# A graph layer on one core: all edge rows scattered in the score stage

## The chip, the core and the metric

The kernel runs on one core of a Trainium2 chip: TensorE (PE, with its weight loads PEld), VectorE (DVE), ScalarE (ACT), GpSimd (POOL) and SyncE (SP), each with its own instruction queue, and 16 DMA engines that all queues share. The metric is the device time of one execution in microseconds, the median of the runs.

## The reference

There are 6250 nodes of 256 features and 200000 edges. An edge goes from a source (`src`, random) to an owner (`dst`, sorted), and carries three times. Layer norms and the typed output layer stand around this core, which is what the stages below compute:

```python
K, Q, V = [typed_linear(x, W, b, node_type) for W, b in ((Wk, bk), (Wq, bq), (Wv, bv))]
e0, e1, e2 = [cos(log(edge_attr[:, i] + 1)[:, None] * w_time + b_time) for i in (0, 1, 2)]
def edge_msgs(Kn, Qn, Vn, ek, eq):
    k = concatenate([Kn, ek], 1).reshape(-1, H, DK)          # H = 4, DK = 56
    q = concatenate([Qn, eq], 1).reshape(-1, H, DK)
    att = einsum('ehd,ed->eh', k, q.sum(axis=1)) / sqrt(DK)
    return att, concatenate([Vn, ek], 1).reshape(-1, H, DK)
att, v = edge_msgs(K[row], Q[col], V[row], e1, e2)           # row = src, col = dst
att_i, v_i = edge_msgs(K[col], Q[row], V[col], e2, e1)
att, att_i = seg_softmax(att, col, n), seg_softmax(att_i, row, n)
res = concatenate([(v * att[:, :, None]).reshape(-1, H * DK), e0], 1)
res_i = concatenate([(v_i * att_i[:, :, None]).reshape(-1, H * DK), e0], 1)
agg = segment_sum(res, col, n) + segment_sum(res_i, row, n)
```

So each edge gives one row of 256 values to the node that it ends in (direction 0) and one to the node that it starts from (direction 1), each weighted by its own softmax.

## The kernel before

Edges are laid out as 1664 tiles of 128. In a tile all edges belong to one group of 128 nodes, so that a sum over a tile is a matmul with a 128x128 one-hot. Work goes in rounds of 8 tiles (`G`), 208 rounds (`NS`) a stage. There are two orders of the edges, one by owner (direction 0) and one by source (direction 1). The stages run one after the other, with a barrier of all engines between them:

- `group_nodes`, `project`: node types, and a table in DRAM with K, Q and V of each node.
- `sort_edges` (`count_owners`, `place_edges`): counts, and for each edge its slot in both orders. The edges' records are scattered to owner order. A record holds also its slot in source order (`SLOT`); unused slots of `bys` are filled with empty rows here, by scatters of `k.padslot`.
- `exchange`, the score stage, works in owner order. A round loads records (SP, L905), gathers the sources' table rows (POOL, L942, eight indirect DMAs of 128 rows of 1888 bytes, into one of three `row` buffers), takes the owners' rows from an SBUF table by matmul (PE, L1062; ACT copies them out, L986 and L987), makes the time embeddings (ACT, L1000 to L1005) and both scores (DVE, L1113 to L1118). SP stores the direction 0 rows to `spill` (L922) and the scores to `runs` (L924). The direction 1 rows, 264 words each with value, scores, source and slot, are collected in `pb`, two buffers, and SP stores them linearly, in owner order, to `mid` (L926).
- `to_runs`, `softmax`, `weights`, `aggregate` for direction 0, then the same four for direction 1. `aggregate` is the sum: SP loads rows (L1446), ACT makes the one-hots (L1487 to L1495), DVE weighs the rows (L1508), PE sums them (L1469), DVE adds to the total (L1518).
- `store_sums`, `output`.

Direction 1 needs its rows by source, in `bys`. In the kernel before, `forward` (L1129) does this, one indirect DMA on POOL for 128 rows, after `mid` has been reloaded: 16 rounds (`AHEAD`) inside the first `softmax`, where ACT issues the loads ahead of its exponentials, and 192 rounds inside the first `aggregate`. There SP first issues the loads of 32 rounds (`LEAD`, L1441) ahead of its own row loads, and then one load a round; from round 160 on there are none left. After round 160 ACT waits for all scatters (`scores_back`) and loads the direction 1 scores, 20 bytes of each of the 212992 rows, in eight DMAs (L1483). Only then does it make the one-hots of the last 48 rounds.

The order of work on each engine is written out by hand; every wait is a semaphore in the engine's queue. In `exchange` POOL's queue is, per round n: wait for the score of round n-1 (`s_sco`), wait for the indices of round n+2 (`s_of`) and for the store of the row buffer (`s_v`), then eight gathers of round n+2. ACT's `owners` waits until the `pb` buffer that it is to fill has been stored (`s_mid`).

Of the kernel before, what the change touches and what calls it, by code (L numbers as in the profile page):

```python
# [8 lines left out]
F32 = mybir.dt.float32  # L9
# [6 lines left out]
P = 128  # L16
# [6 lines left out]
class Sizes:  # L23


    def __init__(self, x, dst, Wk, Wa, w_time):
# [37 lines left out]
        self.AHEAD = 16  # L64
        self.LEAD = 32
# [340 lines left out]
def sort_edges(nc, k, S, src, dst, edge_attr, recs, otile1, bys):  # L406
# [3 lines left out]
    with ExitStack() as ctx:  # L410
        s = Scope(nc, ctx, "sort")
        own = s.sb("own", [P, 2, CT])
# [430 lines left out]
def exchange(nc, k, S, w_time, b_time, table, recs, spill, mid, runs):  # L843
# [16 lines left out]
    with ExitStack() as ctx:  # L860
# [7 lines left out]
        pb = [s.sb(f"pb{n}", [P, G, RC]) for n in range(2)]  # L868
# [9 lines left out]
        prod = s.sb("prod", [P, G, H, DK])  # L878
# [7 lines left out]
        s_u, s_tu, s_fr, s_as, s_mid = [[s.sem(f"{n}{h}") for h in range(2)] for n in ("u", "tu", "fr", "as", "mid")]  # L886
        s_row, s_v = [[s.sem(f"{n}{h}") for h in range(R)] for n in ("row", "v")]
# [14 lines left out]
        def _(sp):  # L902
# [13 lines left out]
            def step(n, i, j, left):  # L916
# [8 lines left out]
                sp.wait_ge(s_sco, n + 1)  # L925
                sp.dma_start(mid[:, bass.ds(n * G, G), :], pb[h][:]).then_inc(s_mid[h], 16)  # L926
            rounds(sp, step)
            for h in range(2):
                sp.wait_ge(s_as[h], 16 * (NS // 2))
                sp.wait_ge(s_mid[h], 16 * (NS // 2))  # L930
# [4 lines left out]
        def _(pool):  # L935
# [9 lines left out]

            def step(n, i, j, left):
                if left >= 2:
                    pool.wait_ge(s_sco, n)
                    gathers(n + 2, i, j + 2)
            gathers(0, 0, 0)  # L950
            gathers(1, 0, 1)
            rounds(pool, step)

        @block.scalar
        def _(act):
# [11 lines left out]
            def owners(n, i, j):  # L967
                h, q = ring(j, 2), ring(j, 4)
                act.wait_ge(s_mid[h], 16 * turn_of(i, j, 2, PER))
                act.wait_ge(s_as[h], 16 * turn_of(i, j, 2, PER))  # L970
                nc.scalar.activation(pb[h][:, :, S.SLOTC].bitcast(I32), rec[q][:, :, S.SLOT].bitcast(I32), ACT.Copy)
                nc.scalar.activation(pb[h][:, :, S.SC + H:S.SC + H + 1], rec[q][:, :, S.SRC:S.SRC + 1], ACT.Copy)
                nc.scalar.activation(at[h][:, :, H:H + 1], rec[q][:, :, S.OWN:S.OWN + 1], ACT.Copy).then_inc(s_own, 1)
# [7 lines left out]
            def gathered(n, j):  # L981
                h = ring(j, 2)
                act.wait_ge(s_sco, n - 1 if not isinstance(n, int) else max(n - 1, 0))
                for t in range(G):
                    act.wait_ge(s_gat, n * G + t + 1)
                    nc.scalar.activation(pb[h][:, t, 0:PROJ], pG[t % 4][:, 0:PROJ], ACT.Copy)  # L986
# [9 lines left out]
            def cosines(n, i, j):  # L996
# [3 lines left out]
                nc.scalar.activation(pb[h][:, :, PROJ:PROJ + 2 * TD], frac[:, :, 0:2 * TD], ACT.Sin, scale=-2 * math.pi)  # L1000
# [79 lines left out]
        def _(dve):  # L1080
            nc.vector.memset(tab[:, NO - 1, :], 0.0).then_inc(s_clr, 1)
            for h in range(2):
                nc.vector.memset(pb[h][:, :, S.RCW:RC], 0.0)
# [14 lines left out]
            def step(n, i, j, left):  # L1098
                h, q = ring(j, 2), ring(j, R)
                link, n_link = chain(dve, s_dve, n * 4)  # L1100
# [11 lines left out]
                dve.wait_ge(s_ev, (n + 1) * G)  # L1112
                link(nc.vector.tensor_tensor(c[:, :, QT:DK], c[:, :, QT:DK], c[:, :, DK + PROJ:QKE], ALU.add))  # L1113
# [5 lines left out]
                assert n_link[0] == 4  # L1119
# [13 lines left out]
def softmax(nc, k, S, d, att_d, keys, alpha_d, mid=None, bys=None):  # L1133
# [5 lines left out]
    with ExitStack() as ctx:  # L1139
# [17 lines left out]
        if bys is not None:  # L1157
            s_turn = s.sem("turn")
            pb = [s.sb(f"pb{n}", [P, S.G, S.RC]) for n in range(8)]
            s_pb, s_sc = [[s.sem(f"{n}{j}") for j in range(8)] for n in ("pb", "sc")]  # L1160
# [40 lines left out]
        @block.gpsimd  # L1201
        def _(pool):
            if bys is not None:
                for n in range(S.AHEAD):
                    pool.wait_ge(s_pb[n % 8], 16 * (n // 8 + 1))
                    pool.sem_inc(s_turn, 1)
                    for t in range(S.G):
                        forward(nc, S, pb[n % 8], t, bys).then_inc(s_sc[n % 8], 16)
                for n in range(8):
                    pool.wait_ge(s_sc[n], 16 * S.G * (S.AHEAD // 8))  # L1210

        @block.scalar
        def _(act):
            if bys is not None:
                for n in range(S.AHEAD):
                    if n >= 8:
                        act.wait_ge(s_sc[n % 8], 16 * S.G * (n // 8))
                    nc.scalar.dma_start(pb[n % 8][:], mid[:, n * S.G:(n + 1) * S.G, :]).then_inc(s_pb[n % 8], 16)
# [166 lines left out]
def aggregate(nc, k, S, s2, d, rows_v, head, al, total, crd=None, mid=None, bys=None):  # L1385
# [16 lines left out]
    ONLY = S.LEAD if bys is not None else 0  # L1402
    SKIP = S.AHEAD if bys is not None else 0
    BOTH = NS - ONLY - SKIP if bys is not None else 0
    if bys is not None:
        pb = [s2.sb(f"pb{n}", [P, G, S.RC]) for n in range(4)]
# [417 lines left out]
```

## Time and profile before

| | us |
|---|---|
| runs, median of 3 | 11923.16 |
| lowest to highest | 11920.98 to 11970.68 |
| profiled execution | 11958.76 |
| its span in the trace | 11956.7 |

```profile
## 1 busy us (share of the span) xinstructions
PE 7581.8 (63%) x33184; PEld 5391.1 (45%) x33185; DVE 6391.6 (53%) x13112; ACT 4234.1 (35%) x12997; POOL 6309.1 (53%) x5432
## 2 busy tenths in 40 slices
PE   3787777777777747777777771034455526499555
PEld 1276666677666633333333331023343314377322
DVE  1096555555555537777777775022233326788533
ACT  0101222222222226666666661022233315488311
POOL 3302555555555548888888885677777760000122
PEclk6655555555555558888898885567677768799755
DMA  1110000000000028888988887567777779588410
```

Section 1 is each engine's busy time. Section 2 cuts the span in 40 slices of 299 us; a digit is the busy share in tenths, and the row PEclk is TensorE's granted clock. Slices 15 to 24 are the score stage, 25 is the first softmax, 26 to 34 the first sum, 35 to 37 the second softmax and sum. POOL counts only while an instruction of it runs; the gap that it needs between two of them is idle time here.

### The profile page before, as it was taken

To read this page: it belongs to the slowest core of one execution; us is meant where nothing else is said; L and a number is where in the kernel's file an instruction comes from. 1 tells how busy PE (TensorE), PEld (TensorE's weight loads), DVE (VectorE), ACT (ScalarE), POOL (GpSimd) and SP (SyncE) were. 2 spreads that over 40 slices of the span, in tenths; PEclk is the share of its full clock that TensorE was granted. 3 is DMA by queue.
4 is the path that set the end of the run, shared out by engine and by line. 5 is a ranking of instruction groups with operands and counts; after the bars stand their busy time and mean duration, and the time that the engine had idled before them with its cause. 6 is when DMAs were issued, how large, how long until landed. Compare 5 with 4: busy or idle time off the path is not lost. (4 is left out here: it accounts for less than half of the span.)

```text
span 11956.7 us, 138038 instructions
## 1 busy us (share of the span) xinstructions
PE 7581.8 (63%) x33184; PEld 5391.1 (45%) x33185; DVE 6391.6 (53%) x13112; ACT 4234.1 (35%) x12997; POOL 6309.1 (53%) x5432
## 2 busy tenths in 40 slices
PE   3787777777777747777777771034455526499555
PEld 1276666677666633333333331023343314377322
DVE  1096555555555537777777775022233326788533
ACT  0101222222222226666666661022233315488311
POOL 3302555555555548888888885677777760000122
PEclk6655555555555558888898885567677768799755
DMA  1110000000000028888988887567777779588410
GB/s 64 36 42 5 6 6 6 6 6 6 6 6 6 6 96 308 308 304 304 306 306 302 304 293 222 179 242 267 256 278 274 272 195 165 175 258 259 157 34 16
DMA packets 1338916, 1878.44 MB, mean 157 GB/s; under 512 B 413200, under 2 KB 1138683, under 8 KB 1285261
## 3 DMA queue, kind: packets, MB, share of 16 engines
q1 hardware_dynamic: 861902, 1184.16, 29.1%
q0 software_dynamic: 261440, 671.33, 17.5%
q10 hardware_dynamic: 215424, 21.56, 2.3%
q14 instruction: 132, 1.08, 0.0%
q8 instruction: 18, 0.29, 0.0%
HBM read 1160.18 MB, written 747.87 MB: 160 GB/s over the span
## 5 line engine op out<-in xcount | busy, mean ns | idle before, releaser
L1469 PE MATMUL sum_pS<-sum_row,sum_oh 128*128 128x260 f32 x6656 | 1854.8, 440 | 1577.1 <-issue 1347.2
L942 POOL DMA_INDIRECT exch_row<-table,exch_of x1664 | 2293.7, 1378 | 625.7 <-issue 549.9
L792 POOL DMA_INDIRECT recs<-place_rec,place_addr x1568 | 1617.6, 1032 | 1572.4 <-DVE place_rec L772 1101.3
L1469 PEld LDWEIGHTS sum_pS<-sum_row,sum_oh 128*128 128x128 f32 x6656 | 1435.6, 221 | 1996.0 <-issue 1737.2
L1129 POOL DMA_INDIRECT bys<-sum_pb x1536 | 1695.0, 1104 | 592.7 <-issue 490.6
L1062 PE MATMUL exch_pG<-exch_tab,exch_ohT 128*128 x3328 | 1607.5, 638 | 475.2 <-ACT exch_kc L987 281.0
L704 PE MATMUL place_pL<-place_cur,place_t_lo 128*128 128x49 f32 x6272 | 1423.7, 409 | 71.8 <-issue 69.2
L1508 DVE TENSOR_TENSOR sum_row<-sum_row,agg_al 128x1792 f32<-128x1792 f32 x416 | 840.7, 2021 | 1165.4 <-DMA sum_row<-spill 850.0
L704 PEld LDWEIGHTS place_pL<-place_cur,place_t_lo 128*128 128x128 f32 x6272 | 1397.0, 332 | 84.5 <-issue 82.1
L1062 PEld LDWEIGHTS exch_pG<-exch_tab,exch_ohT 128*128 128x128 f32 x3328 | 722.4, 227 | 1331.0 <-issue 1330.0
L752 DVE SCALAR_TENSOR_TENSOR place_junk<-place_pB,place_own_g,sort_tri 128x128 bf16<-128x128 f32 x3136 | 887.9, 346 | 289.6 <-DMA table<-proj_kv,proj_idx 261.8
L1495 ACT ACTIVATE sum_oh<-sum_off 128x1024 f32<-128x1024 f32 x416 | 439.6, 1057 | 1686.5 <-DMA soft_key<-keys 794.8
L1491 ACT ACTIVATE sum_off<-kept_ramp,sum_neg 128x128 f32<-128x128 f32 x3328 | 1017.5, 388 | 0.0
L760 DVE TENSOR_TENSOR place_prod<-place_pL,sort_oh_hi 128x392 f32<-128x392 f32 x392 | 345.0, 880 | 1111.3 <-remote 863.6
L643 ACT ACTIVATE place_t_lo<-place_pT 128x1024 f32<-128x1024 bf16 x392 | 399.4, 1019 | 1426.3 <-remote 1288.8
L1619 POOL MEMSET out_xr<- 128x1024 f32 x2 | 1.8, 951 | 1399.3 <-POOLq L112 1399.3
L695 PE MATMUL place_pB<-place_rows,sort_sel 64*128 64x128 bf16 x3136 | 469.0, 301 | 369.4 <-issue 369.4
L1518 DVE TENSOR_TENSOR edge_acc<-edge_acc,sum_pS 128x260 f32 x832 | 351.7, 423 | 653.0 <-DMA soft_key<-keys 279.2
L986 ACT ACTIVATE exch_pb<-exch_pG 128x192 f32<-128x192 f32 x1664 | 562.3, 338 | 274.5 <-PE exch_pG L1062 179.4
L987 ACT ACTIVATE exch_kc<-exch_pG 128x248 f32<-128x248 f32 x1664 | 641.9, 386 | 0.0
L708 PE MATMUL place_pC<-sort_oh_hi,sort_oh_lo 128*128 128x49 bf16 x3136 | 425.2, 276 | 213.9 <-issue 204.7
L647 ACT ACTIVATE place_cur<-place_pC 128x392 f32<-128x392 f32 x394 | 195.2, 496 | 1007.5 <-PE place_pC L708 528.5
(290 smaller groups left out, 11019.2 us busy)
## 6 DMA issues: line engine op xcount, KB each, us to landing
mid<-exch_pb SPq DMA_DIRECT2D x208, 1056.0 KB
spill<-exch_row SPq DMA_DIRECT2D x208, 1024.0 KB
sum_row<-spill SPq DMA_DIRECT2D x208, 1024.0 KB
sum_row<-bys SPq DMA_DIRECT2D x208, 1024.0 KB
sum_pb<-mid SPq DMA_DIRECT2D x192, 1056.0 KB
exch_row<-table,exch_of POOLq DMA_INDIRECT x1664
recs<-place_rec,place_addr POOLq DMA_INDIRECT x1568
bys<-sum_pb POOLq DMA_INDIRECT x1536
```

Of the source, the lines that this page charges most:

```text
L695: last = nc.tensor.matmul(pB[b][:, t, :], sel[:, u % 2 * 16 + u // 2 * LN + 4 * b + t, :], rows[:, par, :], start=True, stop=True)
L704: last = nc.tensor.matmul(pL[u % 2][:, t * NO:(t + 1) * NO], t_lo[:, u % 2, t, :], cur[:, d, t * NO:(t + 1) * NO], start=True, stop=True)
L752: last = nc.vector.scalar_tensor_tensor(out=junk[:, b, t, :], in0=pB[b][:, t, :], scalar=own_g[:, par, d, c:c + 1], in1=tri[:], op0=ALU.is ...
L792: nc.gpsimd.indirect_dma_start(recs, bass.IndirectOffsetOnAxis(addr[:, par, 0, t:t + 1], 0), rec[:, par, t, :], None, bounds_check=P * NT - 1,
L942: nc.gpsimd.indirect_dma_start(row[q][:, t, TD:TD + S.TW], None, table, bass.IndirectOffsetOnAxis(of[q][:, t:t + 1], 0), bounds_check=N - ...
L986: nc.scalar.activation(pb[h][:, t, 0:PROJ], pG[t % 4][:, 0:PROJ], ACT.Copy)
L987: nc.scalar.activation(kc[h][:, t, 0:DK + PROJ], pG[t % 4][:, PROJ:GW], ACT.Copy).then_inc(s_ev, 1)
L1062: nc.tensor.matmul(pG[t % 4][:, 0:GW], ohT[:, t, :], flat[:, bass.ds(tiles[t] * GW, GW)], start=True, stop=True).then_inc(s_gat, 1)
L1129: return nc.gpsimd.indirect_dma_start(bys, bass.IndirectOffsetOnAxis(pb[:, t, S.SLOTC:S.SLOTC + 1].bitcast(I32), 0), pb[:, t, :], None, bo ...
L1469: last = nc.tensor.matmul(pS[h * HG + t // 2][:, 0:AW], oh[h][:, t, :], row[j][:, t, :], start=(t % 2 == 0), stop=(t % 2 == 1))
L1491: last = nc.scalar.activation(off[:, t, :], k.ramp[:], ACT.Abs, bias=neg[h][:, t:t + 1])
L1508: nc.vector.tensor_tensor(r, r, bc(al[:, bass.ds(n * G, G), :], 3, DK), ALU.mult).then_inc(s_w, 1)
```

## The change

The rows are no longer stored to `mid`. In `exchange`, POOL scatters each round's `pb` to `bys` itself: in its round n it issues the gathers of round n+2, waits for the score of round n and issues eight scatters. `pb` has three buffers, and ACT's `owners` waits until the scatters of the round that used its buffer last have landed (`s_fwd`). The tile `prod` is gone: the products are written over their inputs. `mid`, its store and its loads are gone, and with them POOL's and ACT's part in the first softmax and POOL's part and the extra loads in the first sum. The loads of the direction 1 scores come at the start of the first sum, ahead of ACT's first round. `k.padslot` is allocated in an inner scope.

```diff
@@ def exchange(... spill, runs, bys):
-        pb = [s.sb(f"pb{n}", [P, G, RC]) for n in range(2)]
+        pb = [s.sb(f"pb{n}", [P, G, RC]) for n in range(R)]
-        prod = s.sb("prod", [P, G, H, DK])
@@ sync
-                sp.wait_ge(s_sco, n + 1)
-                sp.dma_start(mid[:, bass.ds(n * G, G), :], pb[h][:]).then_inc(s_mid[h], 16)
@@ gpsimd
+            def scatters(n, q):
+                pool.wait_ge(s_sco, n + 1)
+                pool.sem_inc(s_turn, 1)
+                for t in range(G):
+                    forward(nc, S, pb[q], t, bys).then_inc(s_fwd[q], 16)
             def step(n, i, j, left):
                 if left >= 2:
                     pool.wait_ge(s_sco, n)
                     gathers(n + 2, i, j + 2)
+                scatters(n, ring(j, R))
+            for q in range(R):
+                pool.wait_ge(s_fwd[q], 16 * G * (-(-(NS - q) // R)))
@@ scalar, owners
-                act.wait_ge(s_mid[h], 16 * turn_of(i, j, 2, PER))
+                act.wait_ge(s_fwd[r], 16 * G * turn_of(i, j, R, PER))
@@ vector
-                link(nc.vector.tensor_tensor(prod[:], rk, bc(c[:, :, 0:DK], 2, H), ALU.mult))
-                nc.vector.tensor_reduce(at[h][:, :, 0:H], prod[:], op=ALU.add, axis=AX).then_inc(s_att, 1)
-                link(nc.vector.tensor_tensor(rq[:, :, QT:DK], rq[:, :, QT:DK], re, ALU.add))
-                link(nc.vector.tensor_tensor(prod[:], ck, bc(rq, 2, H), ALU.mult))
-                nc.vector.tensor_reduce(pb[h][:, :, S.SC:S.SC + H], prod[:], op=ALU.add, axis=AX).then_inc(s_sco, 1)
+                link(nc.vector.tensor_tensor(rk, rk, bc(c[:, :, 0:DK], 2, H), ALU.mult))
+                nc.vector.tensor_reduce(at[h][:, :, 0:H], rk, op=ALU.add, axis=AX).then_inc(s_att, 1)
+                link(nc.vector.tensor_tensor(ck, ck, bc(rq, 2, H), ALU.mult))
+                nc.vector.tensor_reduce(pb[q][:, :, S.SC:S.SC + H], ck, op=ALU.add, axis=AX).then_inc(s_sco, 1)
@@ def softmax
-                    for t in range(S.G):
-                        forward(nc, S, pb[n % 8], t, bys).then_inc(s_sc[n % 8], 16)
...
-                    nc.scalar.dma_start(pb[n % 8][:], mid[:, n * S.G:(n + 1) * S.G, :]).then_inc(s_pb[n % 8], 16)
@@ def aggregate
-                    for t in range(G):
-                        forward(nc, S, pb[j], t, bys).then_inc(s_sc[j], 16)
...
-            sp.dma_start(pb[j][:], mid[:, bass.ds(n * G, G), :]).then_inc(s_pb[j], 16)
...
-                for j in range(4):
-                    act.wait_ge(s_sc[j], 16 * G * ((NS - SKIP) // 4))
-                for a in range(0, NT, NT // 8):
-                    nc.scalar.dma_start(crd[:, a:a + NT // 8, :], v[:, a:a + NT // 8, S.SC:S.SC + H + 1]).then_inc(s_x, 16)
+        if bys is not None:
+            v = bys.rearrange("(p c) f -> p c f", p=P)
+            for a in range(0, NT, NT // 8):
+                nc.scalar.dma_start(crd[:, a:a + NT // 8, :], v[:, a:a + NT // 8, S.SC:S.SC + H + 1]).then_inc(s_x, 16)
```

## Rows read from the trace of the kernel before

**Rows 1.** Windows: from:to, span, busy PE, PEld, DVE, ACT, POOL, then PEclk, DMA share, GB/s.

```profile
4372.00:7285.00 2913.00, 2064.79 (x6032) 1010.13 (x6032) 2162.32 (x1872) 1791.48 (x6238) 2293.70 (x1664) 0.86 0.88 298
...
7321.00:7545.00 224.00, 2.02 (x6) 0.68 (x6) 82.47 (x44) 7.31 (x5) 169.80 (x128) 0.50 0.53 189
...
7571.00:7890.00 319.00, 0.00 (x0) 0.00 (x0) 10.90 (x2) 9.95 (x32) 224.68 (x231) 0.50 0.59 205
7890.00:9826.00 1936.00, 886.17 (x2560) 674.51 (x2560) 584.05 (x802) 571.30 (x1728) 1470.33 (x1306) 0.71 0.76 262
9826.00:9946.00 120.00, 0.00 (x0) 0.00 (x0) 0.00 (x0) 3.30 (x11) 0.00 (x0) 0.50 1.73 32
9946.00:10157.00 211.00, 182.46 (x768) 143.81 (x768) 180.93 (x244) 171.28 (x518) 0.00 (x0) 0.96 0.82 221
...
10181.00:10287.00 106.00, 2.02 (x6) 0.68 (x6) 82.33 (x44) 6.36 (x4) 0.00 (x0) 0.50 0.26 72
...
10312.00:11201.00 889.00, 786.14 (x3328) 617.27 (x3328) 779.50 (x1050) 756.15 (x2289) 0.00 (x0) 0.97 0.79 245
```

**Rows 2.** Groups of POOL: busy us, mean ns of one, idle before and its releasers.

```profile
L942 POOL DMA_INDIRECT exch_row<-table,exch_of x1664 | 2293.7, 1378 | 625.7 <-issue 549.9 <-DMA spill<-exch_row 41.0 <-ACT exch_of L965 34.8
L1129 POOL DMA_INDIRECT bys<-sum_pb x1536 | 1695.0, 1104 | 592.7 <-issue 490.6 <-DMA sum_pb<-mid 102.2
```

**Rows 3.** Timeline, one exchange round: start us, length us, engine, line, idle before.

```profile
5502.05 2.05 DVE L1114 TENSOR_TENSOR exch_prod<-exch_row,exch_kc 128x1792 f32<-128x1792 f32 x1
...
5503.35 1.63 POOL L942 DMA_INDIRECT exch_row<-table,exch_of  x1 [0.30 <-issue]
...
5506.07 0.42 DVE L1116 TENSOR_TENSOR exch_row<-exch_row 128x256 f32<-128x256 f32 x1
...
5506.52 2.03 DVE L1117 TENSOR_TENSOR exch_prod<-exch_kc,exch_row 128x1792 f32<-128x1792 f32 x1
...
5506.58 2.84 POOL L942 DMA_INDIRECT exch_row<-table,exch_of  x1 [0.30 <-issue]
...
5509.72 1.00 POOL L942 DMA_INDIRECT exch_row<-table,exch_of  x1 [0.30 <-issue]
...
5510.52 0.68 DVE L1089 TENSOR_TENSOR exch_oh<-exch_lob,kept_ramp 128x1024 bf16<-128x1024 bf16 x1
```

**Rows 4.** Timeline, scatters of the first sum with DVE idle.

```profile
9786.94 0.97 POOL L1129 DMA_INDIRECT bys<-sum_pb  x1 [0.30 <-issue]
9788.22 0.98 POOL L1129 DMA_INDIRECT bys<-sum_pb  x1 [0.30 <-issue]
```

**Rows 5.** Timeline, end of the exchange and first load behind it.

```profile
7258.35 1.00 POOL L942 DMA_INDIRECT exch_row<-table,exch_of  x1 [0.30 <-issue]
...
7277.83 2.02 DVE L1118 TENSOR_REDUCE exch_pb<-exch_prod 128x32 f32<-128x1792 f32 x1
...
7285.12 0.36 SPq L1294 DMA_DIRECT2D runs_crd<-runs  x1
```

**Rows 6.** The softmax's exponentials: idle time of ACT before them, both softmaxes.

```profile
  DMA bys<-soft_pb: 144.9, 1
```

**Rows 7.** Timeline, start of the first sum: SP's queue, then DVE's first multiplication.

```profile
7571.41 312.11 SPq L1438 DMA_DIRECT2D sum_pb<-mid  x32
...
7892.79 2.02 DVE L1508 TENSOR_TENSOR sum_row<-sum_row,agg_al 128x1792 f32<-128x1792 f32 x1 [308.13 <-DMA sum_row<-spill]
```

**Rows 8.** Timeline, the score loads in the first sum and ACT behind them.

```profile
9826.24 116.14 ACTq L1483 DMA_DIRECT2D runs_crd<-bys  x8
9942.58 0.21 ACT L1487 ACTIVATE sum_neg<-edge_lo 128x8 f32 x1 [216.89 <-issue]
```

**Rows 9.** Timeline, second sum: first matmuls, and the addition at its end.

```profile
10328.03 17.14 PE L1469 MATMUL sum_pS<-sum_row,sum_oh 128*128 128x260 f32 x63 [16.59 <-DVE sum_row L1508]
...
11187.12 13.29 DVE L1539 TENSOR_TENSOR acc_acc<-acc_acc,edge_acc 128x10976 f32<-128x10976 f32 x2
```

More of the change, by code:

```diff
@@ L840, in turn_of, with exchange @@
     return (period // size) * i + j // size
-def exchange(nc, k, S, w_time, b_time, table, recs, spill, mid, runs):
+def exchange(nc, k, S, w_time, b_time, table, recs, spill, runs, bys):
     NT, G, DK, PROJ, TD, H, NO, N, RC, REC = S.NT, S.G, S.DK, S.PROJ, S.TD, S.H, S.NO, S.N, S.RC, S.REC
@@ L1081, in _ @@
             nc.vector.memset(tab[:, NO - 1, :], 0.0).then_inc(s_clr, 1)
-            for h in range(2):
-                nc.vector.memset(pb[h][:, :, S.RCW:RC], 0.0)
+            for q in range(R):
+                nc.vector.memset(pb[q][:, :, S.RCW:RC], 0.0)
             def own_one_hots(n, j):
@@ L1400, in aggregate, with rounds @@
     block = s2.ctx.enter_context(nc.Block())
[L1402 to L1406, printed above, removed]
-        s_pb, s_sc = [[s2.sem(f"{n}{j}") for j in range(4)] for n in ("pb", "sc")]
-        s_turn = s2.sem("turn")
-    def rounds(eng, step, middle=None):
-        if BOTH:
-            with eng.Fori(0, BOTH // 4) as i:
-                for j in range(4):
-                    step(4 * i + j, j, i, 5)
-        if middle is not None:
-            middle()
-        with eng.Fori(BOTH // 4, NS // 4 - 1) as i:
+    def rounds(eng, step):
+        with eng.Fori(0, NS // 4 - 1) as i:
             for j in range(4):
@@ L1422, in rounds @@
             step(NS - 4 + j, j, NS // 4 - 1, 3 - j)
-    @block.gpsimd
-    def _(pool):
-        if bys is not None:
-            with pool.Fori(0, (NS - SKIP) // 4) as i:
-                for j in range(4):
-                    pool.wait_ge(s_pb[j], 16 * (i + 1))
-                    pool.sem_inc(s_turn, 1)
-                    for t in range(G):
-                        forward(nc, S, pb[j], t, bys).then_inc(s_sc[j], 16)
     @block.sync
     def _(sp):
-        def passed(n, j, i):
-            sp.wait_ge(s_sc[j], 16 * G * i)
-            sp.dma_start(pb[j][:], mid[:, bass.ds(n * G, G), :]).then_inc(s_pb[j], 16)
-        if bys is not None:
-            with sp.Fori(0, ONLY // 4) as i:
-                for j in range(4):
-                    passed(4 * i + j + SKIP, j, i)
         def load(n, j):
@@ L1495, in step @@
             nc.scalar.activation(oh[h][:], off[:], ACT.Relu, bias=1.0, scale=-1.0).then_inc(s_oh, 1)
-        rounds(act, step, scores_back)
+        rounds(act, step)
         if bys is not None:
@@ L1767, in gnn_resnorm @@
             Scope.retire(nc)
-            exchange(nc, k, S, w_time, b_time, table, recs, spill, mid, runs)
+            exchange(nc, k, S, w_time, b_time, table, recs, spill, runs, bys)
             Scope.retire(nc)
```

57 lines of the change are left out of this document (16 added, 41 removed).

## The prediction

> **What bounds the kernel now.** I read the stages first: the table of windows, cut at the first and last instruction of each stage [rows 1]. Look at the POOL column. In the exchange (the score stage) POOL is busy for 2294 of 2913 us, in the first sum for 1695 of 2586 us, in the second sum for nothing at all, and the second sum does the same arithmetic in 889 us. So the first sum does not run at the speed of its own arithmetic.
>
> The groups of instructions say what POOL does: in both stages it only issues indirect DMAs, eight per round, and each stands with a mean length and an idle time before it [rows 2]. For the exchange's gathers that is 1.378 us busy plus 625.7 us of idle over 1664 of them. The same row's list of what ended that idle time puts 549.9 us of it on plain issue, that is a gap of some 0.30 us between any two of them, and only 41.0 us on a wait for a transfer. POOL's sequencer never rests: the exchange is bound by the rate at which POOL issues DMAs, and DMA engines (0.88 share), DVE (2162 us, 10.4 a round) and ACT (1791 us, 8.6 a round) lie under it [rows 1].
>
> The timeline of one round shows what one issue costs [rows 3]. Most take 1.00 us and 0.30 of gap. Those that stand beside a long DVE tensor_tensor, with both inputs in SBUF (L1114, L1117), take 1.63 and 2.84 us; beside a reduce they take 1.00. Over the 1664 gathers (1.378 - 1.00) x 1664 = 629 us are spent so, 3.02 us a round. Where DVE does nothing, scatters follow each other every 0.98 + 0.30 = 1.28 us [rows 4].
>
> **What is removed.** Three pieces of the path go.
>
> Softmax: 224 us before, against 106 us for the second softmax, which has the same code without scatters [rows 1]. In the first one ACT's exponentials are queued behind its loads, which wait for scatters to land [rows 6], and the stage ends only when the last of 128 scatters has landed. I price it as the second: 118 us saved.
>
> First sum: SP issues 32 rounds of loads for the scatters before the first row load, each fourth one held by a scatter. That takes 312 us, and DVE's first multiplication comes after 308 us of idle [rows 7]. Then come 1936 us at the scatters' pace, 120 us in which PE and DVE do nothing, and 211 us for the last 48 rounds [rows 1]. All of it is 319 + 1936 + 120 + 211 = 2586 us. After the change I price this stage by the second sum: 889 us, less 13.3 us for the addition of the first sum's result, which only the second has [rows 9]. One thing does not go: the eight loads of scores hold ACT for 116.1 us while it issues them [rows 8], and they now stand ahead of ACT's first one-hot. ACT needs about 4 us more for that one-hot, so PE starts at 120 us of the stage where in the second sum it starts at 10328 - 10312 = 16 us [rows 9]: 104 us on the path. The stage becomes 889 - 13 + 104 = 980 us, so 1606 us saved. The tail of these loads lands within the first rounds beside row loads, as it did before; I take nothing for it, and up to 100 us if row loads starve under it.
>
> The linear store of the rows (L926) and its reload were not on the path themselves. The store is SP's; its removal takes one wait from SP's queue and frees nothing that anyone waits for while POOL is the bound. Its bytes stay in the exchange, as scatters. The memset of one buffer more, the smaller number of DVE links and the in-place products are hidden under POOL and are taken at nothing; without that cover they would be below 1 us a round. Together 118 + 1606 = 1724 us go.
>
> **What is added.** 1664 scatters in the exchange, behind the gathers on POOL. Each costs 1.28 us [rows 4], so 1664 x 1.28 = 2130 us, all on the path, since POOL is the bound already. What the DVE adds to POOL's instructions goes by DVE's instructions, not by POOL's: one round has the same tensor_tensors as before, so I keep the 3.02 us a round and add none. Bounds, from the same round [rows 3]: nothing, if no instruction of POOL is ever caught; 5.6 us a round if the whole length of all five tensor_tensors (2.05 + 2.03 + 0.42 + 0.42 + 0.68) counts. In between, that L1114 cost 0.63 and that L1117 1.84 us. The scatters of the first sum are the nearest row: (1.104 - 0.98) x 1536 = 190 us over the 160 multiplications of 2.02 us that ran beside them (208 rounds less 48) [rows 2, 4, 7], 1.2 each, not far from 3.02 for a round with two. I keep 3.02, since it is the same DVE code beside a POOL that issues without a pause. The round becomes 8 x 1.30 + 8 x 1.28 + 3.02 = 23.7 us.
>
> New waits. POOL waits for the score of round n before scattering it. Behind that wait are the gathers of round n+3, and behind those everything. The score of round n needs gathers issued two rounds earlier, and ACT's buffer of three rounds back. With rounds of 23.7 us, ACT (8.6) and DVE (10.4) begin round n when gathers n and scatters n-3 have landed, which is about 13 us into POOL's round n-2, and are done some 20 us later. POOL asks for the score 12 us into its round n, 46 us after those gathers. The slack is over 25 us, so I take the wait at nothing; each us by which I am wrong costs 208 us. The ACT wait on scatters of three rounds back has the same slack. The waits on the row store (41.0 us [rows 2]) disappear in longer rounds.
>
> The end: the last gather is issued at 7259.4 [rows 5]. Take off 41, add 2130: POOL's last scatter is out at 9348. The last score is ready 20.5 us after the last gather, just when POOL has issued the two rounds of scatters in between, so nothing is added. With 5 us to land, as between the last store and the next stage now, the next stage starts at 9353 instead of 7285: 2068 us added.
>
> **The sum.** 2068 - 1724 = +344 us. On the profiled execution's 11958.8 us this makes 12303. The three runs shown have their median at 11923.2, 0.3% under the profiled one; the difference carries over, so 11923 + 344 = 12267, and I say 12265, a slowdown of 2.9%. In one sentence: the scatters cost POOL the same 1.28 us wherever they stand; before, they covered a sum of some 870 us and part of a softmax, and in the exchange they cover nothing, because POOL was already the bound there.
>
> **A rule about the lock.** POOL's instruction stands at 2.84 us when it starts with a DVE tensor_tensor of 2.03 [rows 3]. The Trainium skill, page "SBUF — State Buffer", section "SBUF: two separate sides", says that GpSimd and a DVE instruction with two SBUF inputs take a shared port pair as an exclusive lock for the whole instruction, and the other fully blocks. By that each of the five would block POOL for its full length if POOL always had a need for the port; the trace agrees in kind, at half the size (3.0 of 5.6 us).
>
> **Rivals.**
> 1. The lock bites in full (the upper bound). With POOL never idle and DVE in no step with it, 5.6 us a round: (5.6 - 3.0) x 208 = +540, so 12805. Against it: POOL was never idle before either. 0.07.
> 2. Faster, by the lock. If scatters, which follow the scores that DVE has just finished, mostly fall where DVE is between tensor_tensors, the 3.02 us shrink. To nothing: 12267 - 629 = 11638. The point from which it decides is 3.02 - 344/208 = 1.37 us a round. For it: rounds get longer and DVE's work does not, and the reduces cost POOL nothing. Against it: POOL issues without a pause, so each tensor_tensor meets some instruction. 0.06; and 0.03 that it ends near no change.
> 3. Faster, since issuing is not a price. If the 1.3 us were backpressure of DMA engines at a 0.88 share and not POOL's own, the exchange would stay at its present length, as its bytes are the same, and 1724 us would be gained: 10199. Against it: 1.28 us also where nothing else moves [rows 4]. 0.03.
>  The Trainium skill, page "DMA: Bandwidth & Descriptors", section "Anatomy of one DMA — SWDGE (gpsimd) path", has this as a rule: descriptor generation is "small, variable", and many descriptors can be emitted before its cost shows. The rows disagree at 128 descriptors an instruction.
> 4. A new wait: POOL stands for the score because ACT and DVE start only once scatters have landed. Fully in series that is 8.6 + 10.4 = 19 us a round, 3950 us, 16215. Against it is the slack above. 0.04.
>
> **How the numbers follow.** The forecast has 0.77, rival 1 0.07, rival 2 0.06 and 0.03 near no change, rival 3 0.03, rival 4 0.04. A measurement of this kernel tells about 0.5% from no change. Faster by more: 0.06 + 0.03 = 0.09. Within: 0.03. Slower: 0.77 + 0.07 + 0.04 = 0.88. The range: the lock at the first sum's 1.2 us a long tensor_tensor, 2.4 a round, gives -129, and with some 40 for the rest 12100; at 1.84 each, 3.68 a round, it gives +137, and with two thirds of the 100 us for the score loads 12470.
>
> **What would show it.** Right: in the exchange, POOL's idle time still almost all issue, a round of 23.7 us, DMA share near half, PE, DVE and ACT busy as long as before in a stage of some 4980 us; softmax near 106; the first sum near 980, its first 120 us with ACT on the score loads; the extra length of POOL's instructions near 630 us in total. Wrong: POOL waiting for the score reduce (rival 4), scatters well off 0.98 us outside DVE's tensor_tensors, or a first sum that keeps the score loads' traffic long after ACT has issued them.

## The result and the profile after

The change makes the kernel slower.

| us | before | after |
|---|---|---|
| median of 4 runs | 11940.95 | 12319.09 |
| lowest to highest | 11920.98 to 11970.68 | 12314.64 to 12321.81 |
| profiled execution | 11958.76 | 12316.63 |
| its span | 11956.7 | 12314.9 |

The ratio is 1.0314, with an interval of 1.0287 to 1.0341. The forecast was 12265 in a range from 12100 to 12470; on the scale of the profiled execution 12303, and 12316.6 was measured. Between the medians the change costs 378 us, against 344 forecast; the medians have no trace, so what follows balances the two profiled executions, which are 358 us apart. The stages of the kernel after, in the view of windows (from:to, span, busy PE, PEld, DVE, ACT and POOL with instructions, PEclk, DMA share, GB/s), are the placement of the edges, the exchange, the first softmax, the first sum and the second sum:

```profile
1017.00:4419.00 3402.00, 2578.65 (x15782) 2302.41 (x15782) 1854.82 (x8041) 683.79 (x1570) 1702.59 (x1670) 0.50 0.03 6
4448.00:9357.00 4909.00, 2344.37 (x6032) 1120.77 (x6032) 2160.59 (x1876) 1803.49 (x6241) 3836.52 (x3328) 0.72 0.58 174
9393.00:9499.00 106.00, 2.02 (x6) 0.68 (x6) 82.31 (x44) 7.38 (x5) 0.00 (x0) 0.50 0.27 72
9525.00:10513.00 988.00, 785.06 (x3328) 616.69 (x3328) 766.24 (x1048) 756.01 (x2288) 0.00 (x0) 0.93 0.95 225
...
10667.00:11555.00 888.00, 786.08 (x3328) 617.41 (x3328) 779.57 (x1050) 756.12 (x2288) 0.00 (x0) 0.97 0.79 246
```

Beside [rows 1], they give the balance. (The exchange is taken to the first load of the next stage; before, that is 4369.5 to 7285.1. The placement of before is in the window under the table.)

| stage | before | after | difference | predicted |
|---|---|---|---|---|
| placement of the edges | 3324 | 3402 | +78 | 0 |
| exchange | 2916 | 4909 | +1993 | +2068 |
| first softmax | 224 | 106 | -118 | -118 |
| first sum | 2586 | 988 | -1598 | -1606 |
| all else | | | +3 | 0 |
| span | 11956.7 | 12314.9 | +358 | +344 |

```profile
1017.00:4341.00 3324.00, 2568.11 (x15782) 2292.47 (x15782) 1853.99 (x8041) 686.93 (x1570) 1717.90 (x1670) 0.50 0.03 6
```

So the total came out 14 us above the forecast by luck: two deviations nearly cancel. The exchange is 75 us cheaper than forecast, and a stage that the change hardly touches is 78 us longer. Both had to be explained; the second is the subject of three experiments below.

POOL's groups in the kernel after (busy us, mean ns of one, idle before and what ended it) answer to [rows 2]:

```profile
L1133 POOL DMA_INDIRECT bys<-exch_pb x1664 | 2106.9, 1266 | 555.0 <-issue 506.5 <-DVE exch_pb L1122 48.5
L937 POOL DMA_INDIRECT exch_row<-table,exch_of x1664 | 1729.6, 1039 | 539.8 <-issue 507.2 <-ACT exch_of L969 32.7
```

Two things are to be seen. Of the idle time only 81 us is not plain issue: behind its first round POOL never rests, now for 4900 us. And the extra length has moved from the gathers (1378 ns before, 1039 now) to the scatters (1266 ns). The view of waits for POOL (total us, times, longest) says what the wait for the score is:

```profile
POOL bys L1133 <- DVE exch_pb L1122: 48.5, 3, 47.9
```

It is one wait of 47.9 us at round 0, before there is any score, and 0.6 us in the 207 rounds behind it. The timeline of one round shows where the extra length comes from, as [rows 3] did for before (start us, length us, engine, line, operation, idle before):

```profile
6518.89 0.97 POOL L1133 DMA_INDIRECT bys<-exch_pb  x1 [0.30 <-issue]
...
6519.60 0.42 DVE L1117 TENSOR_TENSOR exch_row<-exch_row 128x256 f32<-128x256 f32 x1
...
6520.38 2.02 DVE L1119 TENSOR_TENSOR exch_row<-exch_row,exch_kc 128x1792 f32<-128x1792 f32 x1
6521.50 1.75 POOL L1133 DMA_INDIRECT bys<-exch_pb  x1 [0.30 <-issue]
6522.44 2.02 DVE L1120 TENSOR_REDUCE exch_at<-exch_row 128x32 f32<-128x1792 f32 x1
6523.56 0.97 POOL L1133 DMA_INDIRECT bys<-exch_pb  x1 [0.30 <-issue]
6524.38 2.02 DVE L1121 TENSOR_TENSOR exch_kc<-exch_kc,exch_row 128x1792 f32<-128x1792 f32 x1
6524.84 2.40 POOL L1133 DMA_INDIRECT bys<-exch_pb  x1 [0.30 <-issue]
6526.43 2.02 DVE L1122 TENSOR_REDUCE exch_pb<-exch_kc 128x32 f32<-128x1792 f32 x1
```

Both long products (L1114 and L1117 before, L1119 and L1121 now) fall beside scatters in this round. A scatter that starts beside a product takes 1.75 or 2.40 us, one beside a reduce 0.97. The short add of L1117 is the one that [rows 3] has as L1116, between the first reduce and the second product; the change issues it ahead of both products.

The start of the first sum, in the timeline:

```profile
9524.65 128.40 ACTq L1429 DMA_DIRECT2D runs_crd<-bys  x8
...
9656.08 1.06 ACT L1441 ACTIVATE sum_oh<-sum_off 128x1024 f32<-128x1024 f32 x1
...
9657.27 16.27 PE L1418 MATMUL sum_pS<-sum_row,sum_oh 128*128 128x260 f32 x64 [133.52 <-ACT sum_oh L1441]
```

ACT issues the eight score loads for 128.4 us (116.1 in [rows 8]), and PE starts 133 us into the stage, where the forecast had 120.

### The profile page after: what moved, and what is told of

Its sections match the earlier page's. It is cut to its first block and busy times, and to the rows that moved or that the text cites. A ratio compares the mean times of both kernels' runs of the same rounds, so it can differ in the third digit from the quotient of the medians.

```text
span 12314.9 us, 136305 instructions
## 1 busy us (share of the span) xinstructions
PE 7593.0 (62%) x33184; PEld 5312.2 (43%) x33185; DVE 6379.9 (52%) x13113; ACT 4242.5 (34%) x12997; POOL 5971.0 (48%) x5432
## 3 DMA queue, kind: packets, MB, share of 16 engines
q14 instruction: 225, 1.84, 0.0%
## 5 line engine op out<-in xcount | busy, mean ns | idle before, releaser
L1066 PE MATMUL exch_pG<-exch_tab,exch_ohT 128*128 x3328 | 1895.6, 730 | 2181.7 <-ACT exch_kc L991 2161.8
L791 POOL DMA_INDIRECT recs<-place_rec,place_addr x1568 | 1602.5, 1022 | 1666.5 <-DVE place_rec L771 1195.9
L1133 POOL DMA_INDIRECT bys<-exch_pb x1664 | 2106.9, 1266 | 555.0 <-issue 506.5
L1066 PEld LDWEIGHTS exch_pG<-exch_tab,exch_ohT 128*128 128x128 f32 x3328 | 834.6, 264 | 3187.4 <-issue 3187.4
L937 POOL DMA_INDIRECT exch_row<-table,exch_of x1664 | 1729.6, 1039 | 539.8 <-issue 507.2
L1418 PE MATMUL sum_pS<-sum_row,sum_oh 128*128 128x260 f32 x6656 | 1571.1, 389 | 262.7 <-ACT sum_oh L1441 135.1
L1418 PEld LDWEIGHTS sum_pS<-sum_row,sum_oh 128*128 128x128 f32 x6656 | 1234.1, 190 | 599.4 <-issue 427.5
L1093 DVE TENSOR_TENSOR exch_oh<-exch_lob,kept_ramp 128x1024 bf16<-128x1024 bf16 x208 | 144.4, 694 | 1495.3 <-issue 738.2
L1099 DVE SCALAR_TENSOR_TENSOR exch_frac<-exch_turns,exch_pX 128x384 f32<-128x384 f32 x208 | 115.2, 554 | 1194.3 <-issue 540.0
L975 ACT ACTIVATE exch_pb<-exch_rec 128x8 int32<-128x8 int32 x208 | 45.2, 217 | 1938.6 <-DMA bys<-exch_pb 1934.4
```

The lines of the kernel that those rows point to most:

```text
L791: nc.gpsimd.indirect_dma_start(recs, bass.IndirectOffsetOnAxis(addr[:, par, 0, t:t + 1], 0), rec[:, par, t, :], None, bounds_check=P * NT - 1,
L937: nc.gpsimd.indirect_dma_start(row[q][:, t, TD:TD + S.TW], None, table, bass.IndirectOffsetOnAxis(of[q][:, t:t + 1], 0), bounds_check=N - ...
L1066: nc.tensor.matmul(pG[t % 4][:, 0:GW], ohT[:, t, :], flat[:, bass.ds(tiles[t] * GW, GW)], start=True, stop=True).then_inc(s_gat, 1)
L1133: return nc.gpsimd.indirect_dma_start(bys, bass.IndirectOffsetOnAxis(pb[:, t, S.SLOTC:S.SLOTC + 1].bitcast(I32), 0), pb[:, t, :], None, bo ...
L1418: last = nc.tensor.matmul(pS[h * HG + t // 2][:, 0:AW], oh[h][:, t, :], row[j][:, t, :], start=(t % 2 == 0), stop=(t % 2 == 1))
```

## The experiments

The comparison above ran on one chip, called the first here; its times match none of the three chips that the experiments ran on, called A, B and C. Each comparison is with the kernel before on the same chip. The kernel before takes 10974.3 us on chip A, 10989.8 on chip B and 12198.4 on chip C.

### The place of `padslot` (chip A)

The only line of the change that touches the placement stage's own buffers is the one that allocates `k.padslot` in an inner scope. This kernel is the one before with that alone:

```diff
+        k.padslot = s.sb("padslot", [P, S.NPC], I32)
-            k.padslot = s2.sb("padslot", [P, S.NPC], I32)
```

> The kernel before with one thing of the change alone: k.padslot is allocated in the inner scope. The placement stage (place_edges, the same code in both kernels) took 3322 us in the trace of before and 3401 us in that of after, 79 us more, which no step of the prediction has. Theory A: the shift of the SBUF addresses does it, then this kernel takes about 79 us more than before (12020) and its placement stage 3400 us. Theory B: it varies from execution to execution, then the time is that of before within 0.4% and the stage may lie anywhere from 3320 to 3400.

Measured: 10978.5 us, ratio 1.0001 [0.9991, 1.0011]. Its windows, placement and first sum:

```profile
1016.00:3451.00 2435.00, 2409.16 (x15782) 2272.80 (x15782) 1831.81 (x8041) 693.43 (x1570) 1723.42 (x1670) 0.50 0.04 8
6676.00:9181.00 2505.00, 1132.93 (x3328) 861.09 (x3328) 777.64 (x1048) 755.50 (x2288) 1699.85 (x1536) 0.70 0.81 249
```

The edit does nothing where this stage takes its short form; it didn't run on a chip where the stage is long. The placement stage takes 2435 us here and 3324 on the first chip, with the same instructions and the same granted clock (0.50).

### The linear store as well (chip A)

The kernel after, with the store to `mid` put back on SP, so that the exchange moves the bytes of both:

```diff
+                sp.wait_ge(s_sco, n + 1)
+                sp.dma_start(mid[:, bass.ds(n * G, G), :], pb[q][:]).then_inc(s_mid[q], 16)
@@ owners
+                act.wait_ge(s_mid[r], 16 * turn_of(i, j, R, PER))
```

> The changed kernel, with the linear store of the rows put back beside the scatters (220 MB more, on SP's queue). Theory: POOL's issue rate is the bound and DMA engines have room (0.54 share), so the exchange stays at 4909 us within 20 us. Rival: bytes are what it waits for, then a round gets longer by about 1.08 MB at 300 GB/s, 3.6 us, 750 us in all.

Measured: 11356.8 us, ratio 1.0347 [1.033, 1.0365]. The window of the exchange:

```profile
3483.00:8406.00 4923.00, 2332.93 (x6032) 1114.04 (x6032) 2160.34 (x1876) 1801.43 (x6241) 3853.21 (x3328) 0.73 0.66 219
```

A quarter more bytes (219 against 174 GB/s) cost 14 us on the 4909 measured on the first chip. Bytes are not the bound, and taking the linear store away gave next to nothing back.

### Without the two long products (chip A)

```diff
-                link(nc.vector.tensor_tensor(rk, rk, bc(c[:, :, 0:DK], 2, H), ALU.mult))
-                link(nc.vector.tensor_tensor(ck, ck, bc(rq, 2, H), ALU.mult))
```

> The changed kernel without the two long multiplications of the scores (DVE L1119, L1121); the reduces run over the unmultiplied values, so the scores are not the reference's. DVE is off the path, so by the rival nothing changes. Theory: these two cost POOL most of its 549 us of extra length (2.6 us a round), so the exchange gets some 500 us shorter: kernel near 11820 us, POOL's indirect DMAs at a mean of 1.00 (gathers) and 0.98 to 1.00 us (scatters).

Measured: 10864.4 us, ratio 0.9901 [0.9881, 0.9921]; its scores are not the right ones, since the products are left out. The exchange, and POOL's groups:

```profile
3479.00:7902.00 4423.00, 2268.62 (x6032) 1093.19 (x6032) 1317.48 (x1460) 1804.17 (x6241) 3356.74 (x3328) 0.75 0.64 193
```

```profile
L937 POOL DMA_INDIRECT exch_row<-table,exch_of x1664 | 1700.0, 1022 | 539.6 <-issue 506.4 <-ACT exch_of L969 33.2
L1131 POOL DMA_INDIRECT bys<-exch_pb x1664 | 1656.7, 996 | 549.3 <-issue 506.3 <-DVE exch_pb L1120 43.1
```

The stage is 486 us shorter than the 4909 with the products. DVE wasn't the bound in it (2161 us busy of 4909), and the stage's length fell by what POOL's instructions lost: the means are 1022 and 996 ns, and POOL's busy time is 3837 - 3357 = 480 us less. Of the 549 us of extra length in the kernel after, the two products cause some 480. Of the other 70, some 40 stand beside short tensor_tensors in this trace; most of the rest are scatters of 1.00 us where the count has 0.975.

### 816 tiny gathers more (chip A)

Four more indirect DMAs a round, in 204 rounds, each of 128 pieces of 4 bytes, into a tile that nobody reads:

```diff
+                if left >= 4:
+                    pool.wait_ge(s_tiny, n * 64)
+                    for t in range(4):
+                        nc.gpsimd.indirect_dma_start(tiny[:, t:t + 1], None, slots,
+                                                     bass.IndirectOffsetOnAxis(k.nodes[:, t:t + 1], 0), ...).then_inc(s_tiny, 16)
```

> The changed kernel with four more indirect DMAs a round on POOL in 204 of the 208 rounds, each a gather of 4 bytes for each of 128 partitions, into a tile that nothing reads. They move 0.4 MB in all. Theory: an issue costs POOL 1.30 us whatever it moves, so the exchange gets 816 x 1.30 = 1060 us longer: kernel near 13380 us. Rival (the length is backpressure of the transfers): less than 100 us.

Measured: 12415.5 us, ratio 1.1315 [1.1292, 1.1337]. The exchange and the three groups:

```profile
3481.00:9461.00 5980.00, 2306.69 (x6032) 1105.94 (x6032) 2160.37 (x1876) 1800.79 (x6241) 4657.29 (x4144) 0.68 0.48 143
```

```profile
L1143 POOL DMA_INDIRECT bys<-exch_pb x1664 | 2117.7, 1273 | 553.9 <-issue 506.8 <-DVE exch_pb L1132 47.1
L939 POOL DMA_INDIRECT exch_row<-table,exch_of x1664 | 1680.2, 1010 | 539.5 <-issue 507.0 <-ACT exch_of L979 32.5
L958 POOL DMA_INDIRECT exch_tiny<-slots,kept_nodes x816 | 859.4, 1053 | 249.0 <-issue 249.0
```

The stage is 5980 - 4909 = 1071 us longer, 1.31 us for each of the 816, although they move 0.4 MB in all and the DMA share fell to 0.48. The price of an indirect DMA here is POOL's, whatever its bytes. (All of them have 128 pieces; whether the price goes by the instruction or by its pieces, no run varied.) The 1053 ns of the tiny ones hold some that a product caught: with DVE idle they stand at 1.00 us in this trace. The rows say one more thing. With 20 instructions a round instead of 16, the extra length is 496 us on the scatters, 17 on the gathers and some 43 on the tiny ones (each mean less 0.975 or 1.00, times the count), 556 us: no more than the 549 with 16. It goes by DVE's instructions, not by the number of POOL's.

### The kernel after once more (chip B)

No edit, to see whether the placement stage is longer with it.

> The changed kernel as it is, beside the kernel before on one chip, in a session in which the placement stage takes some 2435 us in all kernels. The stages that the change touches, from the start of the exchange to the start of the second softmax, went from 5811 to 6089 us in the first traces. If the 79 us of the placement stage there belonged to those executions and not to the change, the difference is now 278 us, not 358. If it belongs to the change, 358.

Measured: 11342.6 us, ratio 1.0327 [1.031, 1.0344], 353 us more than before. Placement, exchange and first sum:

```profile
1016.00:3450.00 2434.00, 2408.75 (x15782) 2271.96 (x15782) 1832.29 (x8041) 693.55 (x1570) 1720.61 (x1670) 0.50 0.04 8
3480.00:8390.00 4910.00, 2321.42 (x6032) 1111.15 (x6032) 2160.77 (x1876) 1803.51 (x6241) 3839.50 (x3328) 0.73 0.58 174
8558.00:9545.00 987.00, 784.62 (x3328) 616.39 (x3328) 766.45 (x1049) 756.04 (x2288) 0.00 (x0) 0.93 0.95 225
```

The placement stage takes 2434 us, as in the kernel before on chip A: in the stage's short form the change adds nothing to it. By the totals alone the expectation would have said the opposite, since 353 is near its 358. The stages explain it: the first sum of the kernel before took 2505 us in the `padslot` run and 2586 on the first chip, so the change had 81 us less to take away. (That 2505 is from chip A; the kernel before has no trace on chip B. With it the stages add up to 358 us.)

### Score loads spread over the rounds (chip B)

The kernel after, with the eight score loads of the first sum replaced by one small load a round on SP:

```diff
+            if bys is not None:
+                sp.dma_start(crd[:, bass.ds(n * G, G), :], bys_v[:, bass.ds(n * G, G), S.SC:S.SC + H + 1]).then_inc(s_x, 16)
-            for a in range(0, NT, NT // 8):
-                nc.scalar.dma_start(crd[:, a:a + NT // 8, :], v[:, a:a + NT // 8, S.SC:S.SC + H + 1]).then_inc(s_x, 16)
```

> The changed kernel, with the score loads of the first sum taken from ACT's queue (eight, 116 us of issue ahead of the first one-hot) and spread over SP's queue, one small load of 1024 pieces of 20 bytes a round. Theory: 104 us of issue stood on the path and their transfer is hidden beside the sum, so the first sum goes from 988 to 884 us, with a few us a round more at most where DMA engines (0.83 share in the second sum, and some 0.15 more here) come near their limit. Rival: the transfers themselves, not their issue, were the cost; then the stage stays above 950 us.

Measured: 11226.3 us, ratio 1.0219 [1.0202, 1.0237], and 116 us less than the kernel after. The first sum:

```profile
8560.00:9430.00 870.00, 785.26 (x3328) 617.49 (x3328) 766.79 (x1048) 755.70 (x2286) 0.00 (x0) 0.98 0.95 256
```

987 - 870 = 117 us were the price of ACT issuing the loads, and the 212992 small pieces themselves cost the stage nothing that can be seen. The expectation had 104 us for the issue, since it took the start of PE from the kernel before. It improves the change and doesn't save it.

### The kernel before, its first sum unblocked (chip B)

Here the order before is kept: the scatters stay in the sum, where they cover it. Only what held the sum up goes: no 32 rounds of loads ahead (`LEAD` 0), and ACT waits for the scatters and loads the scores after its last one-hot instead of before the last 48 rounds.

```diff
-        self.LEAD = 32
+        self.LEAD = 0
@@ sync
-        if bys is not None:
+        if bys is not None and ONLY:
@@ scalar
-        rounds(act, step, scores_back)
+        rounds(act, step)
+        scores_back()
```

> The kernel before, with two changes of order in the first sum: no loads of 32 rounds for the scatters ahead of the row loads (LEAD = 0), and ACT loads the scores after its last one-hot and not before the last 48 rounds. Theory: POOL's issue is the bound of exchange and first sum; in the latter it has 1536 scatters, 2250 us, and whatever of the sum is done beside them is free. Before, 48 rounds (211 us) came behind them. Now 16 rounds at most do, beside the score loads, so the stage goes from 2586 to about 2250 + 150 + 15 = 2415 us and the kernel gets 170 us faster than before (ratio 0.985). Rival: the row loads come late behind the scatters' loads in SP's queue and slow POOL; then no gain.

Measured: 10858.2 us, ratio 0.9883 [0.9867, 0.99]: 1.2% faster than the kernel before and clear of the interval, near the 0.985 expected, and 0.957 of the kernel after's time on the same chip. The first sum, in two windows, and the load in the timeline:

```profile
6683.00:8942.00 2259.00, 1192.87 (x3328) 903.78 (x3328) 765.02 (x1040) 755.43 (x2289) 1758.56 (x1536) 0.73 0.80 274
8942.00:9078.00 136.00, 0.00 (x0) 0.00 (x0) 14.54 (x9) 0.00 (x0) 0.00 (x0) 0.51 1.75 31
```

```profile
8942.65 115.91 ACTq L1483 DMA_DIRECT2D runs_crd<-bys  x8
```

All 3328 matmuls of the sum are done beside 1536 scatters in 2259 us, and only the score loads stand alone behind them. The stage takes 2395 us, 110 less than the 2505 of the `padslot` run; the medians differ by 132, and the rest I can't place (the profiled execution was the longest of the four, 10885.5).

### Both kernels on a third chip (chip C)

No edit in either; to see what the two stages that vary do on a chip where the kernel before is slow.

> The kernel before, a third look. The placement stage took 3322 us (before) and 3401 us (after) in the first traces and 2435 us in five kernels of the second session, before and after alike. Theory: that is a state of the chip or of the session, the same for both kernels, with a scatter of its own in the slow state; then this one and the next agree within 2 us if the stage takes 2435 us, and may differ by tens of us if it takes over 3300. Rival: the change lengthens it by 79 us; then the next one has it again. The first sum took 2586 and 2505 us in two traces of this kernel; a third value between 2490 and 2600 says that some 80 us of it vary.

> The changed kernel beside it: placement stage as said there; exchange 4909 us within 5, first softmax 106, first sum 988 within 3, since POOL's issue, and then DVE and PE, set them and no transfer does.

Measured: 12196.5 us for the kernel before, ratio 0.9995 [0.9983, 1.0007] with itself, and 12460.5 for the kernel after, ratio 1.022 [1.0186, 1.0254]. Placement and first sum of the kernel before:

```profile
1017.00:4545.00 3528.00, 2607.08 (x15782) 2306.21 (x15782) 1852.64 (x8041) 682.36 (x1570) 1700.76 (x1670) 0.50 0.03 6
7766.00:10396.00 2630.00, 1014.52 (x3328) 781.59 (x3328) 775.43 (x1048) 756.07 (x2289) 1684.44 (x1536) 0.69 0.77 237
```

Placement, exchange and first sum of the kernel after:

```profile
1017.00:4572.00 3555.00, 2612.19 (x15782) 2305.03 (x15782) 1851.52 (x8041) 684.05 (x1570) 1701.72 (x1670) 0.50 0.03 6
4602.00:9518.00 4916.00, 2390.06 (x6032) 1134.78 (x6032) 2162.04 (x1876) 1814.49 (x6241) 3844.95 (x3328) 0.72 0.58 174
9685.00:10672.00 987.00, 784.97 (x3328) 616.63 (x3328) 766.38 (x1048) 758.53 (x2288) 0.00 (x0) 0.93 0.95 225
```

The exchange (4909, 4910, 4916) and the first sum (988, 987, 987) of the kernel after agree within 7 us on every chip (4916 is 2 us outside what was expected). What varies is the placement, in both kernels, and the first sum of the kernel before: 2505, 2586 and now 2630 us, which is outside the expected 2490 to 2600. The variation shows in POOL's scatters, above all in one wait: the time spent on a wait for `mid` to be loaded is 102.2 us on the first chip [rows 2], 39.8 in the `padslot` run on chip A and 153.4 on chip C:

```profile
L1130 POOL DMA_INDIRECT bys<-sum_pb x1536 | 1699.8, 1107 | 507.4 <-issue 467.6 <-DMA sum_pb<-mid 39.8
```

```profile
L1129 POOL DMA_INDIRECT bys<-sum_pb x1536 | 1684.4, 1097 | 647.8 <-issue 494.4 <-DMA sum_pb<-mid 153.4
```

Against the first chip the waits differ by 62 and 51 us and the stages by 81 and 44. With the rest of the same rows, busy time and idle time on plain issue, the group takes 2288 us on the first chip, 2207 on chip A and 2332 on chip C, and that is the whole of both differences. So the change gains most in the first sum where the kernel before waits most for its reload, and its loss is least there: on chip C, where the placement is 27 us longer with it, the ratio is 1.022.

## Why the prediction was right

**The bound, right and shown.** The forecast stands on POOL paying for each indirect DMA and not for its bytes. The tiny gathers show it (1.31 us each for 512 bytes), and the added store shows the other half (a quarter more bytes for 14 us). Rival 3, that issuing is not a price, falls with both: 10199 would have needed an exchange of unchanged length. The Trainium skill's rule weighed there (page "DMA: Bandwidth & Descriptors", section "Anatomy of one DMA — SWDGE (gpsimd) path"), that descriptor generation is small and that many can be emitted before it shows, is no guide here: with DVE idle POOL is held for 1.00 us and a gap of 0.30 by 128 pieces of 4 bytes as by 128 of 1888, and that bounds the stage. How the time goes with the number of pieces no run shows.

**1.28 us a scatter, right.** Scatters beside no product stand at 0.97 to 1.00 us with a gap of 0.30 in the exchange as in [rows 4], although 174 GB/s move beside them.

**The lock's extra length, mis-sized.** "I keep the 3.02 us a round and add none" was the term that was off. Measured are (1.039 - 1.00) x 1664 = 65 us on the gathers and (1.266 - 0.975) x 1664 = 484 us on the scatters, 549 us or 2.64 a round, against 629. The 80 us are the larger part of what the exchange came out under the forecast: POOL's busy time grew by 88 us less than forecast (the 80, and 8 since a scatter stands at 0.975 and not 0.98), its idle time on plain issue by 35 us less (the gathers' fell from 549.9 to 507.2), and 48 us of a wait at the start came on top; -88 - 35 + 48 = -75. The rows for it had been there: the first sum's scatters gave 1.2 us a product [rows 2], and taking the two products away released 480 / 208 / 2 = 1.15 us each. I had kept 3.02 because it was "the same DVE code". It isn't the same, and the traces say what that does.

An instruction of POOL that starts while a product runs ends some 0.85 us after the product's end, wherever it started. In [rows 3] that is 5504.98 - 5504.10 = 0.88 and 5509.42 - 5508.55 = 0.87, in the round above 0.85 and 0.84; over the exchange the medians are 0.87 us before and 0.85 after, and nearly all lie between 0.84 and 0.92. Alone it takes 0.97 or 1.00. So a product costs POOL its own length, less what has run of it when POOL's instruction starts, less some 0.13 (1.00 - 0.87): 2.03 - 0.06 - 0.13 = 1.84 us for the second product before, and 2.02 - 0.46 - 0.13 = 1.43 now.

The moment moved because the short add left its place between the two products: the second starts 1.98 us after the end of the first (6524.38 - 6522.40) and no longer 2.42 (5506.52 - 5504.10), while POOL, which the first product holds and releases, starts its next but one instruction 2.44 us after that end now, 2.48 before. This is so in 203 of 208 rounds before and in 207 after, and the second product cost POOL 372 us before and 296 after, which is 76 of the 80. (The first fell by 41, all else rose by 37.) In the first sum of the kernel before POOL's instructions start at any moment of the product, from 0.1 to 1.2 us into it. With half of POOL's step of 1.30 us as the mean, that gives an estimate of 2.02 - 0.65 - 0.13 = 1.24 us a product, and 1.2 was measured. No run moved the add alone, so this is read from the traces and not tried.

The sign that it goes by DVE's instructions and not by POOL's was right (556 us with 20 instructions a round, 549 with 16). The Trainium skill's rule on a port that the two engines share as a lock, where the other fully blocks (page "SBUF — State Buffer", section "SBUF: two separate sides"), fits the trace better than the prediction's "half the size" says: an instruction of POOL that a product catches waits until the product has ended. What keeps the sum under 5.6 us a round is that an instruction of POOL that has started before a product ends in its usual time (beside the product at 5502.05 of [rows 3] it takes 0.99 us), and that short tensor_tensors often fall wholly beside such a one. Scatters that start beside a reduce stand at 0.97 us.

**Rivals 1 and 2.** Both were about this term. Fully blocked would be 5.6 us a round; 2.64 was measured. For the time to come out unchanged on chip B, 353 / 208 = 1.70 of the 2.64 would have had to go. Without the products, which took 480 us from the stage, the kernel ran at 0.9901. So the products' price is large enough to turn the sign. It doesn't go by itself when scatters follow scores: 80 us went, and by the traces the moved add did that, not rival 2's reason. (The two kernels of that ratio differ in the products too, so it isn't the change's own.)

**The new wait, right.** Rival 4 wanted 19 us in every round; behind the first round the waits have 0.6 us in all, and so the slack of over 25 us held. The start was overlooked: at round 0 POOL waits 47.9 us for the first score. The 41.0 us on the row store that the forecast took off [rows 2] did go, so the start gave them back.

**Softmax, right** (106, as forecast). **First sum, nearly** (988 for 980): the score loads stood in ACT's queue for 128 us and not 116, so PE started 13 us later than forecast, and rounds behind them gave 5 us back. The fear that their traffic starves row loads was empty: with the loads spread the sum takes 870 us, 117 less, which is what their issue held PE up by, and no more.

**Placement, not forecast.** Where the stage is short it takes 2435 and 2434 us in the one and the other kernel, and `padslot` alone does nothing (1.0001), so there the change has no part in it. Where the stage is long, two pairs of traces have it 78 and 27 us longer with the change. That the change does this in the long form is neither shown nor excluded: `padslot` alone wasn't run there, and the 378 us between the medians of the first comparison say that the profiled pair was no outlier. The prediction had put this stage at nothing. Without the 78 us the forecast would have been high by 64 us instead of low by 14, and most of that is the lock. It would still have lain well within the range.

**What stays open.** Why the placement stage takes 2435 us in the traces of chips A and B and 3324 to 3555 in those of the first chip and chip C, and whether the change adds to the long form. In its long form ACT and DVE stand in it for a releaser that the profile calls remote, in the kernel before on the first chip:

```profile
ACT place_t_lo L643 <- remote: 1288.8, 175, 10.9
DVE place_prod L760 <- remote: 863.6, 182, 15.3
```

The three other traces with the long form, of the kernel after and of both kernels on chip C, have such waits too. Where the stage is short (the `padslot` run, the kernel after on chip B) the view has none at all. Whether the waits for `mid`, short on chip A and long on chip C, have the same root, and whether the chip decides or the moment, can't be told from these runs.

## What to carry to other kernels

Count what a step issues on the engine that issues it, and ask in which stage that engine has time left: 1664 scatters cost POOL 1.28 us each wherever they stand, apart from what DVE adds, and they were moved from a sum of some 870 us, which they covered, to a stage where POOL was the bound already and they cover nothing, so that saved bytes and saved loads didn't matter. Where such work covers another stage badly, repair the cover first: with a handful of lines changed the sum ran wholly beside the scatters, for 0.9883 where the move cost 1.0327 on the same chip. And price the mutual slowing of two engines from the moments at which they meet: here a short add left the gap between two products, and what the second costs the other engine fell from 1.84 to 1.43 us. Where the moments are unknown, take a range from every stage in which the two meet.

## What the runs showed of the hardware that was not expected

- An indirect DMA of 128 pieces of 4 bytes holds POOL for 1.00 us and a gap of 0.30 where VectorE is idle, as much as one of 1888-byte rows (1.00 us in the same run).
- A VectorE product of two SBUF operands of 2.02 us, beside a POOL that issues without a pause, costs POOL 1.15 us on average (480 us for 416 products). A POOL instruction that starts during it ends 0.84 to 0.92 us after it, wherever it started, against 0.97 or 1.00 us alone.
- Eight loads of 26624 pieces of 20 bytes hold the issuing ACT for 116 to 128 us, although one small load a round for the same pieces on SP costs the stage nothing that can be seen.
- The same code with the same granted clock takes 2435 us on one chip and 3528 on another in one stage, while the exchange of the kernel after, bound by POOL's issuing, agrees within 0.2% (4909 to 4916).
